# A graph-attention edge loop on one core: one operand of the message product and of the one-hot is read from PSUM

## The reference

```python
xn = layernorm(x)
h = einsum('ni,hio->hno', xn, W)                 # 4 heads of 64
e = leaky(attn_src[:, src] + attn_dst[:, dst]) * edge_weight
e_exp = exp(e - max(e))
denom = segment_sum(e_exp, dst)
out = segment_sum(h[:, src] * e_exp / denom[dst], dst)
x = x + out + mixer(xn)                          # linear attention, 4 heads of 32
x = x + ffn_on_top_half_of_tokens(layernorm(x))
```

## Time and profile before

| | |
|---|---|
| median of three runs | 868.28 us (868.2 to 870.37) |
| the profiled execution: span | 864.6 us |
| median less that span | 3.7 us |
| PE, DVE, POOL, ACT busy | 709.8, 596.9, 513.7, 231.3 us |
| gathers (line 380) | 392, 419.3 us busy |
| message products (line 930) | 98, 119.8 us busy |
| one-hots (line 992) | 98, 67.4 us busy |

### The profile page before, as it was taken

The page is one execution under the profiler, slowest core; times in us unless marked ns, Lnnn a source line. Parts: engine busy times, 40 slices in busy tenths (PEclk is TensorE's granted clock), DMA queues, the critical chain, the costliest instruction groups (busy, mean ns, idle before and its releaser), DMA issues.

```text
span 864.6 us, 18704 instructions
## 1 busy us (share of the span) xinstructions
PE 709.8 (82%) x4369; PEld 541.9 (63%) x4370; DVE 596.9 (69%) x1630; ACT 231.3 (27%) x915; POOL 513.7 (59%) x512
## 2 busy tenths in 40 slices
PE   3799687887878798868787878787876998999995
PEld 2576665555555565545565546465555987999994
DVE  7665277565657576657675757676667991999985
ACT  1133502111212122213132323232333442333331
POOL 5242537777777777778777777777751070333332
PEclk9899799776769776777787868787787998999998
DMA  6254325554556555554555545555420002000000
GB/s 202 69 170 80 95 59 132 128 123 121 123 125 129 125 124 129 121 124 119 122 128 128 128 115 126 126 119 120 115 79 1 1 1 78 19 31 26 32 25 21
DMA packets 104859, 82.97 MB, mean 96 GB/s; under 512 B 67133, under 2 KB 91566, under 8 KB 104561
## 3 DMA queue, kind: packets, MB, share of 16 engines
q0 software_dynamic: 18816, 52.21, 22.6%
q1 hardware_dynamic: 85873, 29.16, 15.6%
HBM read 74.47 MB, written 6.84 MB: 94 GB/s over the span
## 4 chain that ended last, share of the span: by engine, by line
POOL 37%; issue 26%; PE 21%; DVE 9%; DMA 4%; SPq 2%; POOLq 1%; DVEq 0%; ACT 0%; ACTq 0%
POOL G L380 37%; PE ps L561 8%; PE ps L574 7%; PE ps L414 2%; PE ps L420 2%; DVE wprod L1086 1%; DMA x<-in_x 1%; DVE G L1069 1%; DVE x L1073 1%; DVE stats L739 1%; DVE x L1027 1%; DMA dstm_d<-wide 1%; DMA htab<-hst 1%; DVE acc L1079 1%; DMA G<-htab,srcr 1%
## 5 line engine op out<-in xcount | busy, mean ns | idle before, releaser
L380 POOL DMA_INDIRECT G<-htab,srcr x392 | 419.3, 1070 | 149.9 <-issue 138.3
L480 PE MATMUL ps<-msg,oh 128*128 128x260 f32 x784 | 303.0, 525 | 74.0 <-DVE oh L992 73.7
L480 PEld LDWEIGHTS ps<-msg,oh 128*128 128x128 f32 x784 | 176.6, 249 | 105.0 <-issue 78.9
L930 DVE TENSOR_TENSOR msg<-G,msg 128x1024 f32<-128x1024 f32 x98 | 119.8, 1222 | 32.8 <-issue 22.2
L561 PEld LDWEIGHTS ps<-xnT,w 128*128 128x128 f32 x800 | 98.3, 201 | 3.8 <-issue 1.8
L561 PE MATMUL ps<-xnT,w 128*128 128x128 f32 x800 | 98.8, 285 | 2.1 <-ACT wide L721 1.6
L663 ACT ACTIVATE negR<-ps 128x1 f32<-128x1 f32 x98 | 16.8, 171 | 291.2 <-PE ps L476 253.9
L574 PE MATMUL ps<-w,wide 128*128 128x256 f32 x400 | 90.4, 379 | 1.0 <-DVE acc L1093 1.0
L393 POOL TENSOR_SCALAR G<-acc,mw 128x256 f32<-128x256 f32 x25 | 23.1, 926 | 99.6 <-DVE mw L1126 90.4
L449 PE MATMUL ps<-ad,ohT 128*128 x1464 | 74.7, 176 | 8.7 <-issue 4.5
L992 DVE TENSOR_TENSOR oh<-iota,dmr 128x512 f32<-128x512 f32 x98 | 67.4, 687 | 19.8 <-issue 19.0
(11 more groups left out here) (137 smaller groups left out, 801.8 us busy)
## 6 DMA issues: line engine op xcount, KB each, us to landing
dstb<-dstu_d SPq DMA_DIRECT2D x98, 128.0 KB
G<-htab,srcr POOLq DMA_INDIRECT x392
htab<-hst SPq DMA_DIRECT2D x25, 130.0 KB, 3.2
out<-G SPq DMA_DIRECT2D x24, 128.0 KB, 1.7
x<-in_x SPq DMA_DIRECT2D x4, 640.0 KB, 8.0
w<-in_L_ffn_w SPq DMA_DIRECT2D x4, 512.0 KB
kq<-w_d SPq DMA_DIRECT2D x1, 1600.0 KB, 6.3
dmr<-dstm_d SPq DMA_DIRECT2D x98, 2.0 KB
```

The source lines that it names most:

```text
L380: gp.indirect_dma_start(G[:, q % RING, k, :], None, htab, bass.IndirectOffsetOnAxis(ap=srcr[:, q, k:k + 1], axis=0)).then_inc(s_g[q % RING ...
L480: m = pe.matmul(ps[:, 3 + p, 0:ROW], oh[:, p, k, :], msg[:, p, k, :], start=(k == 0), stop=(k == TILES - 1))
L930: dve.tensor_tensor(msg[:, p, :, 0:HF].rearrange("p k (h o) -> p k h o", h=HEADS), G[:, q % RING, :, 0:HF].rearrange("p k (h o) -> p k h o ...
```

## The change

ScalarE writes the exponentials twice, first into msg as before, then into a small tensor exq in PSUM bank 7 (two slots of 16 columns); the semaphore comes with the second. The message product reads them from exq. The iota row is copied once into PSUM bank 7 (`iotap`, 128 columns), after the mixer's context has been taken from that bank, and the one-hot of line 992 reads it there. As bank 7 now holds these, the mixer's last step goes through three banks in place of four. Two waits on the copy (`iota_taken`) are added, one ahead of ScalarE's loop and one ahead of VectorE's. The gathers and their code are the same.

```diff
+        exq = ps[:, 7, 256:256 + 8 * TILES].rearrange("p (s k h) -> p s k h", s=2, k=TILES)
+        iotap = ps[:, 7, 384:512]
...
-        TURN_BANKS, MIX_BANKS = (3, 4, 6), (3, 4, 6, 7)
+        TURN_BANKS, MIX_BANKS = (3, 4, 6), (3, 4, 6)
...
-                if t >= 4:
-                    pe.wait_ge(S["mix_added"], t - 3)
-                pe.matmul(ps[:, MIX_BANKS[t % 4], 0:D], kq[:, 1, t * P:(t + 1) * P], C2[:, :], start=True, stop=True).then_inc(S["mix_multiplied"], 1)
+                if t >= 3:
+                    pe.wait_ge(S["mix_added"], t - 2)
+                pe.matmul(ps[:, MIX_BANKS[t % 3], 0:D], kq[:, 1, t * P:(t + 1) * P], C2[:, :], start=True, stop=True).then_inc(S["mix_multiplied"], 1)
...
-                act.activation(msg[:, p, :, HF:ROW], et[:, p, 0:16].rearrange("p (k h) -> p k h", k=TILES), ACT.Exp, bias=negR[:, p:p + 1]).then_inc(S["exp_ready"], 1)
+                e = et[:, p, 0:16].rearrange("p (k h) -> p k h", k=TILES)
+                act.activation(msg[:, p, :, HF:ROW], e, ACT.Exp, bias=negR[:, p:p + 1])
+                act.activation(exq[:, p, :, :], e, ACT.Exp, bias=negR[:, p:p + 1]).then_inc(S["exp_ready"], 1)
...
+            act.wait_ge(S["iota_taken"], 1)
             groups(step)(act)
...
-                ex = msg[:, p, :, HF:ROW].unsqueeze(3).to_broadcast([P, TILES, HEADS, OUT_F])
+                ex = exq[:, p, :, :].unsqueeze(3).to_broadcast([P, TILES, HEADS, OUT_F])
...
-                    dve.tensor_tensor(oh[:, q % 2, :, :], iota[:, :].unsqueeze(1).to_broadcast([P, TILES, P]),
+                    dve.tensor_tensor(oh[:, q % 2, :, :], iotap.unsqueeze(1).to_broadcast([P, TILES, P]),
...
+            dve.tensor_copy(iotap, iota[:, :]).then_inc(S["iota_taken"], 1)
             dve.wait_ge(S["c2_multiplied"], 1)
...
-                dve.tensor_tensor(x[:, t, :], ps[:, MIX_BANKS[t % 4], 0:D], x[:, t, :], ALU.add).then_inc(S["mix_added"], 1)
+                dve.tensor_tensor(x[:, t, :], ps[:, MIX_BANKS[t % 3], 0:D], x[:, t, :], ALU.add).then_inc(S["mix_added"], 1)
...
+            dve.wait_ge(S["iota_taken"], 1)
```

More of the change, by code:

```diff
@@ L188, in gps_layer @@
                      "xn2_ready xn2_turned xn2T_ready hidden_ready gelu_ready y_ready y_taken out_staged "
-                     "split_steps acc_zeroed").split():
+                     "split_steps acc_zeroed iota_taken").split():
             S[name] = sem("s_" + name)
```

## The result

The changed kernel takes 830.19 us, median of 4 runs (824.77 to 832.06), against 868.26 for the kernel before; the ratio is estimated as 0.9578, 95% interval 0.9539 to 0.9617 (the two medians alone would give 0.9561). Forecast were 835, range 824 to 854. An execution over 1.5% longer than the fastest of its kernel counts as slow and is left out of the ratios, and in the run with three gathers and sixteen groups to a turn, where it is one of four, out of the time too. The profiled execution took 831.26 us with a span of 829.2.

The account below looks back on a forecast made before the run. POOL's gathers, lengthened beside two-SBUF-input VectorE instructions, were taken as the loop's bound. 94 x (5.515 - 5.15) = 34.3 us gained, 0.5 given back in the mixer: -33.8, from 868.28 to about 835 us; range 824 to 854.

Parts of the forecast that it names:

- POOL as the only bound of the loop: Edge loop before the change: POOL issues 94 groups of four gathers in 518.4 us, 5.515 us each, without one real wait.
- What the two operands remove: Gathers started inside message product or one-hot: one operand in PSUM removes the overlap delay, about 44 us of POOL.
- The instructions themselves: Message product and one-hot, 98 each: length unchanged with one input in PSUM, bounds 0 and +0.005 us each, taken as 0.
- The second exponential: On ScalarE between max_spread and exp_ready, 98 times: adds 0.1 us; lower bound 0.07 us, upper bound 308 ns.
- The new bound: Loop after the change: serial chain 5.15 us a group, just above POOL's 5.06, so the two share the bound.
- The rate of a free-running group: Serial chain from product to next product without turn stalls: 4.65 us taken, between 4.40 and 4.90, plus 0.1 for the exponential.
- The other signs: Line 380's mean near 0.96 us, VectorE's 69.5 us row wait more than halved, ScalarE wait up from 10 us, among others.
- the turn of the loop: Stall charged once per eight groups: 3.2 us added to 8 x 4.65, giving 40.4 us, 5.05 a group.
- The mixer: Last mixer step, three banks in place of four, 25 steps: 0.5 us given back, bounds 0 and 1.5.
- No effect: Rival, 6%: the operand's place does not matter to the gather; POOL stays at 5.5 us a group, 869 us.
- a serial chain longer than the gathers were: Rival, 7%: second exponential fully exposed at exp_ready, 0.31 us a group, 5.61 us a group, +9 us, 877 us.
- The full gain: Rival, 22%: POOL stays the only bound, the whole 44 us come, 824.7 us; a denser loop may get more 2.4 GHz.

Follow-up runs that it names:

- product only: Changed kernel with the one-hot's iota row taken from SBUF again, the message product still reading PSUM: 833.42 us, 0.9586 of the kernel before.
- one-hot only: Changed kernel with the message product's exponentials taken from SBUF again, the one-hot still reading PSUM: 859.54 us, 0.9901 of the kernel before.

## Why the prediction was right, point by point

**The bound.** POOL as the only bound of the loop, from the fixed 0.30 us between gathers and the one real wait, holds: with three gathers in four the kernel before falls by 5.3%, and with turns of sixteen it hardly moves.

**What the two operands remove.** The forecast took 44 us off POOL. Its busy time fell by 47.1 us (419.3 to 372.2), practically all that stood above the plain length (to 374.9 in the second profiled execution). The prediction's 95 gathers with 40.0 us inside products are 101 with 42.4 in the whole trace, which changes nothing in the argument. Each operand removes its own part and leaves the other's, in one execution (product only, one-hot only). The inference of the Trainium skill, SBUF — State Buffer, section "Who interferes with whom", that a VectorE product of two SBUF tensors leaves descriptor generation alone, doesn't hold for this indirect gather as a whole: 86 of 102 gathers lose 43.1 us inside it in the run with both operands in SBUF, none of 86 loses anything with one in PSUM. The same section's rule on a GpSimd instruction that reads SBUF describes what product and one-hot do to it. That the reading in question is that of the row indices is argued from the fact that a held gather ends 0.82 us after the other instruction, 0.13 less than its plain length, so it is held near its start; no run took the index reading away. Nor did a run move the exponentials into another SBUF tensor: for the product the place and the tensor changed together, and the one-hot, where only the place of the same row changed, speaks for the place.

**What the reading of the lines missed.** The prediction tells the instructions apart by two tensor inputs in SBUF, and says that a gather that meets neither product nor one-hot is plain. The transposed one-hot (line 864, now 870) has one tensor input in SBUF and holds gathers too: before, 13 of the 36 that start inside one are longer, by 1.2 us, and the same goes on in the changed kernel, 7 of 34. In these two traces every gather that starts 0.10 to 0.20 us into it is held, 20 in all, and ends 0.82 us after it:

```profile
394.31 0.35 DVE L870 TENSOR_SCALAR ohT<-dstb,nodeid 128x512 bf16<-128x512 uint16 x1
394.42 1.06 POOL L383 DMA_INDIRECT G<-htab,srcr  x1 [0.30 <-issue]
```

So the number of SBUF inputs is not the whole condition; what this instruction shares with the product no run shows. It is short (0.35 us), so little is lost. Here and at the updates that read hst lies nearly all that is left in the changed kernel, 1.7 us.

**The instructions themselves.** Forecast 0 and measured so: 1222 to 1216 and 687 to 687 ns.

**The second exponential.** The term of 0.1 us was too small. The two start at 206.81 and 207.03, the second takes 258 ns, so exp_ready comes 0.17 us later than the first would have given it; the bounds of 0.07 and 0.31 held it. Of that the pace shows little, the 0.02 us of the runs with three gathers. The trace of the changed kernel around them, ScalarE:

```profile
206.81 0.31 ACT L671 ACTIVATE msg<-et,negR 128x16 f32<-128x16 f32 x1
...
207.03 0.26 ACT L672 ACTIVATE ps<-et,negR 128x16 f32<-128x16 f32 x1
```

**The new bound.** That chain and POOL would come close to each other was right, as the runs with three gathers and with turns of sixteen show from both sides. The order was not: 5.15 was forecast for the chain, above POOL's 5.06; measured are 4.94 for the chain alone and 5.01 for POOL alone, 5.08 together. The rate of a free-running group was forecast as 4.65 + 0.1 = 4.75 us. The 97 intervals between products without their stalls give the same, (490.0 - 29.4) / 97 = 4.75, but they hold 12.9 us of waiting for rows; with three gathers they are 4.64, (479.1 - 29.5) / 97. The sign named for this, real waits of POOL of 0.5 us or more a group, did not come: they are 0.07 a group. The other signs came.

**The term that was off** is the turn of the loop. "8 x 4.65 + 3.2" charges a stall for every eighth group, 94 / 8 = 11.75 of them, 37.6 us. The first eight groups and the last ten are written out, and the ten turns have nine branches back: 9 stalls, 29.4 us. The trace before would have told it: nine stalls of 2.8 to 3.6 us on the timeline, 28.4 us, two of them put down to ScalarE, which is why the page has only 22.2 us of issue before the product. With nine of 3.2 us the forecast's own chain comes to 94 x 4.75 + 28.8 = 475.3 us, no more than POOL's 475, and the sum to 826; 829 to 830 was measured. In the other direction, the sum ended at the last gather, and there the chain is now 3.4 us further behind than it was; that step was missing from it.

**How near the number is, and why.** In spans the forecast was 831 and the profiled execution has 829.2. The loop gained 40.5 us and not 34.3; outside it 5.1 us were given back and not 0.5. The two errors cancel but for 1.6 us, and that is luck.

**The mixer.** 0.5 us given back: not visible.

**The rivals.** No effect, and a serial chain longer than the gathers were, are both excluded, by the trace and by the ratio. The full gain is nearly there in the loop (40.5 us over the 94 groups, where the rival has 43 to 44 and the forecast 34.3), but not in the time; as to the loop, the rival described it better than the forecast. Its argument from the clock did not hold for this stretch: that from 400 to 500 us has more matmul instructions than before, 549 in place of 513, at a granted clock of 0.74 in place of 0.80 (columns as in the earlier trace rows).

```profile
400.00:500.00 100.00, 85.28 (x549) 58.70 (x548) 70.10 (x203) 30.40 (x139) 73.49 (x78) 0.74 0.58 132
```

## What to carry to other kernels

If gathers issued by GpSimd set the pace, look at the distribution of their lengths and at which VectorE instruction each long one started in; an instruction with two SBUF inputs that runs beside them is worth a PSUM home for the smaller, repeated operand, here 16 words and 128 words a partition. Write such a copy first and the other second, if the consumer of the copy is on the chain; here that was probably worth 0.5%. And when one engine is freed, count the stalls of the next one one by one on the timeline, not by the period of the code, and set the pace that each engine has by itself beside the other before saying which is the bound.

## What was not expected of the hardware

The coupling works the other way too, for another instruction. The transposed one-hot (128x512 from uint16 to bf16, one tensor input in SBUF) usually takes 0.35 us, and sometimes 0.40 to 0.60. The changed kernel, POOL and VectorE:

```profile
206.46 0.95 POOL L383 DMA_INDIRECT G<-htab,srcr  x1 [0.30 <-issue]
...
207.00 0.52 DVE L870 TENSOR_SCALAR ohT<-dstb,nodeid 128x512 bf16<-128x512 uint16 x1
```

It starts 0.54 us after the gather and is 0.17 us late. In the two traces of before and after, 25 and 25 of 122 take over 0.40 us, some 4 us too much in all each; all but three of these start 0.46 to 0.74 us after a gather's start, and none that starts in its first 0.4 us is lengthened. It changes nothing between the two kernels.

Products and one-hots with two inputs in SBUF are not lengthened there: in the kernel before 17 products and 12 one-hots start 0.46 to 0.70 us after a gather's start, the longest of them 1.23 and 0.69 us. Nor are the 35 products that start 0.02 to 0.40 us after a gather's start. So they meet a gather near its start only, and when the two start together the gather goes first: five gathers of the kernel before start 0.01 to 0.02 us after a product's start; none is held, and the product takes 1.27 us in place of 1.22:

```profile
369.13 1.27 DVE L930 TENSOR_TENSOR msg<-G,msg 128x1024 f32<-128x1024 f32 x1
369.15 0.94 POOL L380 DMA_INDIRECT G<-htab,srcr  x1 [0.30 <-issue]
```

In the changed kernel, with one input in PSUM, the five such products take 1.20 to 1.22 us.
